# Finishing the rows of two steps' blocks together in the first attention pass of a graph network, and the edge attribute products through two buffers

## Chip, cores and metric

One core of a Trainium2 chip runs the whole program. The metric is the device time of one execution in microseconds; the time before is the median of three runs.

## The reference

A network of four graph layers on 3,125 nodes with 128 features: a graph attention layer with edge attributes, a relational layer, two transformer convolutions, and a two-layer graph convolution. The change touches the first alone. With H = 4 heads of C = 32 columns, E = 103,125 edges, sorted by target, it computes:

```
alpha = leaky_relu(a_src[src] + a_dst[dst] + a_edge, 0.2)     # a_edge from 13 edge attributes
        (and one loop edge per node; its attribute is the mean over the node's edges)
alpha = exp(alpha - segment_max(alpha, dst))
out   = segment_sum(alpha * h[src], dst) / (segment_sum(alpha, dst) + 1e-16)
y     = layernorm(out + bias + x) * gamma + beta
x     = layernorm(x + relu(y))
```

## The kernel before

Nodes lie in NB = 26 blocks of BN = 121 rows, one row to a partition. `attention_pass` is called twice; the first call, named `e0`, has `gat=True` and is the one that the change concerns (the second, `e21`, shares the function). It works in steps. A step takes a chunk of T = 33 tiles of 128 edges, all for one block. With these inputs every block fits one step, so there are 26 steps. Each engine has a loop over 13 pairs of steps, whose body has the two steps u = 0 and u = 1 written out; step s = 2i + u. Here "even step" is u = 0 and "odd step" is u = 1.

In a step the engines do this, tied by semaphores:

- GpSimd (L554) gathers the source rows, 33 indirect DMAs of 128 rows, into `G[:, u]`. There are two such buffers, one per parity of the step. The 33 tiles are in nine batches (`BATCH`); a batch of the step after next may be gathered once TensorE has summed the same batch of this step (`slots_free`).
- SyncE loads the target numbers (`dst3`, and `dstb` over all partitions) and the attributes (`attr`) of the next step once `prepare` of this one is done, and the source numbers of the step after next once the scores are made.
- ScalarE makes the transposed one-hot matrix `OT` of the next step (`one_hot`, L607 and L609) behind the exponential of this step's scores (L617).
- TensorE runs, in this order of its program: the target part of the scores `psQ` of step s (L571, 33 tiles, needs `OT`), six small transposes `psT` (L583), two more `psB` (L588), then the 33 sums `psA` (L594, which need VectorE's weighted rows, L835), and then the `psQ` of step s + 1.
- VectorE waits for the nine gathered batches and for `psQ`, and adds the scores (L790 is the first such instruction of a step). It makes segmented maxima with two scans, subtracts them, weights the gathered rows (L835, nine instructions), runs `prepare` for the next step (L742 to L762), makes the next one-hot matrix `O` (`match`, L766), takes over `psA` (L842), and merges it with the running state `ST` (L845 to L862).

`prepare` ends with the attribute products: for each of four heads a multiplication of 33 x 13 attributes by that head's weights into `pr` (L758) and a sum over 13 (L760), with a drain behind each of the eight.

At the end of each step `finish_block` (L669 to L717) turns `ST` into finished rows of the block: the loop edge's score, the exponential (ScalarE L624), the root for the degree (ScalarE L627), the division, bias, the first `norm` (L648 to L660), gamma, beta, relu, the second `norm`, and the last scaling into `xo[:, u]` (L717). ScalarE takes the roots of both norms, and then stores the rows to the table in memory (L632), after the store before it has landed. Nearly every VectorE instruction there is followed by a drain, since each needs the result of the one before. In a step beyond the last edge or of a block with several steps the same code runs again on the same block.

Of the kernel before, what the change touches and what calls it, by code (L numbers as in the profile page):

```python
# [27 lines left out]
D = 128  # L28
BN = 121
# [413 lines left out]
def attention_pass(g, name, table, width, H, gat):  # L443
# [9 lines left out]
    with ExitStack() as ctx:  # L453
# [28 lines left out]
        if gat:  # L482
            attr = sb("attr", [128, T, 13], F32)
            wed = sb("wed", [128, 13, D])
            atte = sb("atte", [128, D])
            we = sb("we", [128, 4, 13])
            pr = sb("pr", [128, T, 13])
            aff = sb("aff", [BN, 3, D])
            fs = sb("fs", [BN, 20])
            fe = sb("fe", [BN, 8])  # L490
            fy = sb("fy", [BN, D])
            ft = sb("ft", [BN, D])
            fm = sb("fm", [BN, 1])
            fv = sb("fv", [BN, 1])
            fc = sb("fc", [BN, 1])
# [106 lines left out]
        @block.scalar  # L602
        def _(act):
            def one_hot(s):

                act.wait_ge(S["edges_in"], s * (16 * n_in) + 16 * n_in)
                nc.scalar.activation(OT[:], dstb[:], ACT.Square, bias=g["off_t"][0:BN, bass.ds(s, 1)], scale=2.0).then_inc(S["squared"], 1)  # L607
                act.wait_ge(S["squared"], s + 1)
                nc.scalar.activation(OT[:], OT[:], ACT.Relu, bias=one[:], scale=-1.0).then_inc(S["targets_ready"], 1)  # L609

            act.wait_ge(S["one_set"], 1)
            one_hot(0)
            with act.Fori(0, g["n_pairs"](act)) as i:
                for u in range(2):
                    s = i * 2 + u
                    act.wait_ge(S["diff_ready"], s + 1)
                    nc.scalar.activation(G[:, u, :, wo:wo + H].rearrange("p t h -> p h t"), A[:], ACT.Exp).then_inc(S["weights_done"], 1)  # L617
                    act.wait_ge(S["ends_turned"], s + 1)
                    one_hot(s + 1)
                    act.wait_ge(S["merge_ready"], s + 1)  # L620
                    nc.scalar.activation(ex[:], mm[:, 0:2 * H], ACT.Exp).then_inc(S["merge_done"], 1)
                    if gat:
                        act.wait_ge(S["exp_wanted"], s + 1)
                        nc.scalar.activation(fe[:], fs[:, 0:8], ACT.Exp).then_inc(S["exp_made"], 1)  # L624
                        for k, x in enumerate((fc, fv, fv)):
                            act.wait_ge(S["root_wanted"], s * 3 + (k + 1))
                            nc.scalar.activation(x[:], x[:], ACT.Sqrt).then_inc(S["rooted"], 1)  # L627
                        blk = act.value_load(g["steps_i"][0:1, bass.ds(s, 1)], min_val=0, max_val=NB - 1)
                        act.wait_ge(S["row_ready"], s + 1)
                        act.wait_ge(row_stored[1 - u], i * 16 + (16 + 16 * u))  # L630
                        act.sem_inc(S["act_waited"], 1)
                        act.dma_start(g["rows_table"].rearrange("(b p) f -> b p f", p=BN)[bass.ds(blk, 1)].rearrange("a p f -> (a p) f"),  # L632
                                      xo[:, u, :]).then_inc(row_stored[u], 16)
            if gat:
                pairs = g["n_pairs"](act)
                for u in range(2):
                    act.wait_ge(row_stored[u], pairs * 16 + 16)
                    act.sem_inc(S["act_waited"], 1)

        @block.vector  # L640
        def _(dve):
            def bc(x, shape):
                return x.broadcast_to(shape)

            def norm(x, s, count):

                dr = dve.drain
                V.tensor_reduce(fm[:], x, AX.X, ALU.add)  # L648
                dr()
# [12 lines left out]

            def finish_block(s, i, u, blk):

                dr = dve.drain
                plain = D + 2 * H + 1
                q = lambda x, lo, hi: x[:, bass.ds(blk, 1), lo:hi].rearrange("p a f -> p (a f)")
                cnt, al, m, den = ST[:, plain + 4:plain + 5], fs[:, 8:12], fs[:, 12:16], fs[:, 16:20]
                V.tensor_copy(g["deg"][:, bass.ds(blk, 1)], cnt)  # L669
# [4 lines left out]
                V.tensor_tensor(al, q(Q, 0, 4), q(Q, 4, 8), ALU.add)  # L674
                dr()
                V.scalar_tensor_tensor(out=al, in0=ST[:, plain:plain + 4], scalar=fm[:], in1=al, op0=ALU.mult, op1=ALU.add)
                dr()
                V.scalar_tensor_tensor(out=al, in0=al, scalar=0.2, in1=al, op0=ALU.mult, op1=ALU.max)
                dr()
                V.tensor_tensor(m, ST[:, D + H:D + 2 * H], al, ALU.max)  # L680
                dr()
                V.tensor_tensor(fs[:, 0:4], ST[:, D + H:D + 2 * H], m, ALU.subtract)
                V.tensor_tensor(fs[:, 4:8], al, m, ALU.subtract).then_inc(S["exp_wanted"], 1)
                dve.wait_ge(S["rooted"], s * 3 + 1)
                V.reciprocal(g["cnt1"][:, bass.ds(blk, 1)], fc[:])
                dve.wait_ge(S["exp_made"], s + 1)
                V.tensor_tensor(den, ST[:, D:D + H], fe[:, 0:4], ALU.mult)
                dr()
                V.tensor_tensor(den, den, fe[:, 4:8], ALU.add)
                dr()  # L690
                V.tensor_scalar(den, den, 1e-16, None, ALU.add)
                dr()
                V.reciprocal(den, den)
                dr()
                V.tensor_tensor(fe[:].rearrange("p (k h) -> p k h", k=2), fe[:].rearrange("p (k h) -> p k h", k=2),
                                bc(den.unsqueeze(1), [BN, 2, H]), ALU.mult)
                dr()
                hc = lambda x: x.rearrange("p (h c) -> p h c", h=H)
                V.tensor_tensor(hc(fy[:]), hc(ST[:, 0:D]), bc(fe[:, 0:4].unsqueeze(2), [BN, H, C]), ALU.mult)
                V.tensor_tensor(hc(ft[:]), hc(q(g["SKIP"], 0, D)), bc(fe[:, 4:8].unsqueeze(2), [BN, H, C]), ALU.mult)  # L700
                dr()
                V.tensor_tensor(fy[:], fy[:], ft[:], ALU.add)
                dr()
                V.tensor_tensor(fy[:], fy[:], aff[:, 0, :], ALU.add)
                dr()
                V.tensor_tensor(fy[:], fy[:], q(g["X"], 0, D), ALU.add)
                dr()
                norm(fy[:], s, 2)
                V.scalar_tensor_tensor(out=fy[:], in0=fy[:], scalar=fv[:], in1=aff[:, 1, :], op0=ALU.mult, op1=ALU.mult)
                dr()  # L710
                V.tensor_tensor(fy[:], fy[:], aff[:, 2, :], ALU.add)
                dr()
                V.scalar_tensor_tensor(out=fy[:], in0=fy[:], scalar=0.0, in1=q(g["X"], 0, D), op0=ALU.max, op1=ALU.add)
                dr()
                norm(fy[:], s, 3)
                dve.wait_ge(row_stored[u], i * 16 + 16)
                V.tensor_scalar(xo[:, u, :], fy[:], fv[:], None, ALU.mult).then_inc(S["row_ready"], 1)  # L717

            V = nc.vector
            if gat:  # L720
# [16 lines left out]
            def prepare(s, u):  # L737
# [2175 lines left out]
```

## Time and profile before

| | |
|---|---|
| median of 3 runs | 4447.06 us (4443.07 to 4447.44) |
| profiled execution | 4448.53 us, its span 4446.7 us |
| TensorE matmul, weight load busy | 2794.7 us (63%), 2572.4 us (58%) |
| VectorE busy | 3090.5 us (70%) |
| ScalarE busy | 1029.7 us (23%) |
| GpSimd busy | 2741.1 us (62%) |
| mean granted clock of TensorE | 0.736 |

The span is that of one execution, from the first to the last instruction. Busy time is an average over stages with different limits, and the pass `e0` is only one of them: its first gather starts at 58.78 us and its last finished rows are made at 1290.38 us. In the timelines a row gives the start, the duration, the engine, the line, the instruction with what it writes and reads, and in brackets how long the engine stood idle before it and what ended that.

### The profile page before, as it was taken

Reading aid. Unit: us, or ns where it says so; the run is one execution under the profiler, and the core shown is the slowest. Engines: PE = TensorE matmul, PEld = TensorE weight load, DVE = VectorE, ACT = ScalarE, POOL = GpSimd, SP = SyncE. Lnnn points to the kernel's source line nnn. Section 1 sums busy time; section 2 is a strip of 40 time slices with the busy share of each in tenths; the row PEclk is TensorE's granted clock in tenths of the full one; section 3 lists DMA queues with packets and bytes.
Section 4 is the critical chain, followed back from the end, with each engine's and each line's share of the span. In section 5 each row is a group of like instructions: output and inputs, shape, how many; then the busy total and the mean of one; then the engine's idle time right before and its main releaser. Section 6 shows DMA issues by size and latency. Waiting matters only on the chain. (4 is left out here: it accounts for less than half of the span.)

```text
span 4446.7 us, 58830 instructions
## 1 busy us (share of the span) xinstructions
PE 2794.7 (63%) x18074; PEld 2572.4 (58%) x18075; DVE 3090.5 (70%) x7364; ACT 1029.7 (23%) x971; POOL 2741.1 (62%) x2657
## 2 busy tenths in 40 slices
PE   2565656566545565555567465766667657996688
PEld 2565646555534555455556365656656546896566
DVE  3777767777776766666665477777777767997445
ACT  2222222222221222222221121221211213442000
POOL 3777777777627777777772377777777742554000
PEclk7665656565667777777778777877777768998799
DMA  4454444444334445554542455656556533451353
GB/s 108 96 113 99 108 99 97 106 95 111 89 78 118 127 127 136 140 136 136 135 127 80 104 149 145 157 143 153 149 147 154 144 95 93 114 116 37 147 138 91
DMA packets 170486, 526.46 MB, mean 118 GB/s; under 512 B 61894, under 2 KB 88866, under 8 KB 157435
## 3 DMA queue, kind: packets, MB, share of 16 engines
q1 hardware_dynamic: 71532, 297.92, 27.3%
q0 software_dynamic: 95296, 224.30, 19.6%
q8 instruction: 96, 1.57, 0.2%
q10 hardware_dynamic: 3432, 1.61, 0.1%
q14 instruction: 130, 1.06, 0.1%
HBM read 456.16 MB, written 67.48 MB: 118 GB/s over the span
## 5 line engine op out<-in xcount | busy, mean ns | idle before, releaser
L554 POOL DMA_INDIRECT e21G<-table,e21src x858 | 856.4, 998 | 392.2 <-issue 257.8
L554 POOL DMA_INDIRECT e0G<-table,e0src x858 | 863.9, 1007 | 340.1 <-issue 249.8
L1469 POOL DMA_INDIRECT t1G<-table,t1idx x806 | 790.7, 981 | 328.6 <-issue 242.5
L1542 PE MATMUL t1psW<-t1CO,t1G 128*128 128x192 f32 x1612 | 426.0, 426 | 315.3 <-issue 296.9
L1542 PEld LDWEIGHTS t1psW<-t1CO,t1G 128*128 128x128 f32 x1612 | 361.6, 253 | 323.1 <-issue 303.4
L578 PE MATMUL e21psQ<-Q,e21OT 121*128 x1716 | 412.1, 407 | 120.0 <-ACT e21OT L609 44.8
L578 PEld LDWEIGHTS e21psQ<-Q,e21OT 121*128 121x128 f32 x1716 | 400.0, 326 | 131.6 <-issue 86.9
L571 PE MATMUL e0psQ<-Q,e0OT 121*128 x1716 | 398.7, 371 | 78.5 <-ACT e0OT L609 42.4
L571 PEld LDWEIGHTS e0psQ<-Q,e0OT 121*128 121x128 f32 x1716 | 396.6, 325 | 84.0 <-issue 84.0
L2208 POOL TENSOR_TENSOR e22Z<-e22Z,e22C 121x847 f32<-121x847 f32 (+1 forms) x104 | 200.2, 1957 | 257.4 <-ACT e22Z L2200 257.4
L594 PE MATMUL e21psA<-e21G,e21O 128*121 128x145 f32 x1716 | 275.5, 332 | 106.1 <-DVE e21G L835 106.1
L594 PEld LDWEIGHTS e21psA<-e21G,e21O 128*121 128x121 f32 x1716 | 270.4, 224 | 107.8 <-issue 107.8
L594 PE MATMUL e0psA<-e0G,e0O 128*121 128x142 f32 x1716 | 269.2, 328 | 79.8 <-DVE e0G L835 79.8
L594 PEld LDWEIGHTS e0psA<-e0G,e0O 128*121 128x121 f32 x1716 | 263.6, 223 | 82.1 <-DVE e0G L835 82.1
L1781 DVE TENSOR_TENSOR t1AT<-t1AT,t1psW 128x192 f32 x186 | 64.9, 349 | 311.7 <-PE t1psW L1542 311.2
L784 DVE TENSOR_TENSOR e21G<-e21psQ,e21G 128x512 f32<-128x512 f32 (+1 forms) x234 | 150.2, 642 | 153.4 <-DMA e21G<-table,e21src 121.2
L1699 DVE TENSOR_TENSOR t1L<-t1psI,RES 128x1089 f16<-128x1089 f32 (+1 forms) x182 | 226.9, 1247 | 0.0
L1504 PEld LDWEIGHTS t1psN<-SKIP,t1L 128*121 128x121 f16 x1586 | 137.5, 167 | 153.9 <-issue 149.2
L1504 PE MATMUL t1psN<-SKIP,t1L 128*121 128x52 f16 x1586 | 143.8, 238 | 125.7 <-issue 124.4
L583 PE MATMUL e0psT<-eye,e0TI 128*4 128x128 f32 x156 | 37.4, 411 | 283.0 <-DVE e0TI L811 283.0
L1662 DVE TENSOR_TENSOR t1CO<-t1OW,t1psC 128x960 f32<-128x960 f32 x186 | 189.8, 1021 | 20.9 <-issue 10.7
L583 PEld LDWEIGHTS e0psT<-eye,e0TI 128*4 128x4 f32 x156 | 15.6, 113 | 294.1 <-DVE e0TI L811 285.3
(423 smaller groups left out, 5432.1 us busy)
## 6 DMA issues: line engine op xcount, KB each, us to landing
e0dstb<-in_dst_p SPq DMA_DIRECT2D x27, 1996.5 KB
e21dstb<-in_dst_p SPq DMA_DIRECT2D x27, 1996.5 KB
e22C<-counts SPq DMA_DIRECT2D x26, 1487.0 KB
llC<-planes SPq DMA_DIRECT2D x52, 743.5 KB
Q<-in_type_p SPq DMA_DIRECT2D x62, 416.0 KB
counts<-X SPq DMA_DIRECT2D x13, 1487.0 KB
planes<-SKIP SPq DMA_DIRECT2D x26, 743.5 KB
counts<-RES SPq DMA_DIRECT2D x13, 1487.0 KB
```

What stands on the lines that cost most here:

```text
L554: nc.gpsimd.indirect_dma_start(out=G[:, u, t, 0:width], out_offset=None, in_=table, in_offset=bass.IndirectOffsetOnAxis(ap=src[:, u, t:t + ...
L571: mmi = nc.tensor.matmul(psQ[:, u, t * QW:(t + 1) * QW], onehot[:, t, :], Q[:, bass.ds(blk, 1), 0:QW].rearrange("p a f -> p (a f)"), start ...
L578: mmi = nc.tensor.matmul(psQ[:, b % 3, j * QW:(j + 1) * QW], onehot[:, t, :], Q[:, bass.ds(blk, 1), 0:QW].rearrange("p a f -> p (a f)"), s ...
L594: mmi = nc.tensor.matmul(psA[0:BN, 0:NC], O[:, t, :], G[:, u, t, vo:vo + NC], start=(t == 0), stop=(t == T - 1))
L784: V.tensor_tensor(G[:, u, t0:t1, 0:D], q, G[:, u, t0:t1, 0:D], ALU.mult).then_inc(S["spread_free"], 1)
L1469: nc.gpsimd.indirect_dma_start(out=G[:, q % 2, t, :], out_offset=None, in_=table, in_offset=bass.IndirectOffsetOnAxis(ap=idx[:, q * GT + t ...
L1504: mmi = nc.tensor.matmul(psN[0:BN, c % 2, i * 2 * NB:(i + 1) * 2 * NB], L[:, c % 2, i, :], K[:, c % 2, i, :], start=True, stop=True)
L1542: mmi = nc.tensor.matmul(psW[:, k % 2, 0:WIN * NBAS], G[:, q % 2, t, :], CO[:, k % 2, i].rearrange("p b w -> p (b w)"), start=(i == 0), st ...
L1662: V.tensor_tensor(CO[:, k % 2, 0:n], OW[:, u, t0:t0 + n, :].unsqueeze(2).broadcast_to([128, n, NBAS, WIN]), made.unsqueeze(3).broadcast_to ...
L1699: V.tensor_tensor(L[:, c % 2, 0:m, :], iol.unsqueeze(1).broadcast_to([128, m, BN]), lb.unsqueeze(2).broadcast_to([128, m, BN]), ALU.is_equ ...
L1781: V.tensor_tensor(to, to, psW[:, k % 2, 0:WIN * NBAS].rearrange("p (b w) -> p b w", b=NBAS), ALU.add).then_inc(S["added"], 1)
L2208: nc.gpsimd.tensor_tensor(Z[:, u, h0:h1, :], Z[:, u, h0:h1, :], C[:, u, h0:h1, :], ALU.mult).then_inc(S["weighted"], 1)
```

## The change

Two edits, both inside `attention_pass` with `gat=True`.

First, `finish_block` becomes `finish_blocks`, called once per pair. At the end of each step VectorE copies `ST` into a half of a new tile `two`. Behind the odd step, after a drain, it loads both block numbers into registers and finishes both blocks. Where operands lie side by side one instruction covers both halves (tiles `fs`, `fd`, `fx`, `fn`, `fe`, `fy`, `ft`, `fm`, `fv`, `fc` get a dimension of 2); where an operand is addressed by block number, or a scalar per row is used, there are two instructions. The fused loop-edge score (L676) becomes a product and a sum, and `cnt1` is now written from `fc` by two copies. ScalarE does one exponential and three roots per pair, and both stores at the end of the odd step.

Second, the attribute products go through two buffers `pr[:, 0]` and `pr[:, 1]`: head h is multiplied and, without a drain between, head h - 1 is summed; one drain follows each such pair, and the last sum has none behind it. In the diff below the removed body of `finish_block`, which is printed above, and the sizes of the other small tiles are left out.

```diff
--- before.py
+++ after.py
@@ -484,15 +484,19 @@
-            pr = sb("pr", [128, T, 13])
+            pr = sb("pr", [128, 2, T, 13])
...
+            two = sb("two", [BN, 2, NC])
+            fs = sb("fs", [BN, 2, 8])
...
@@ -619,16 +623,18 @@
                     one_hot(s + 1)
                     act.wait_ge(S["merge_ready"], s + 1)
                     nc.scalar.activation(ex[:], mm[:, 0:2 * H], ACT.Exp).then_inc(S["merge_done"], 1)
-                    if gat:
-                        act.wait_ge(S["exp_wanted"], s + 1)
-                        nc.scalar.activation(fe[:], fs[:, 0:8], ACT.Exp).then_inc(S["exp_made"], 1)
-                        for k, x in enumerate((fc, fv, fv)):
-                            act.wait_ge(S["root_wanted"], s * 3 + (k + 1))
-                            nc.scalar.activation(x[:], x[:], ACT.Sqrt).then_inc(S["rooted"], 1)
-                        blk = act.value_load(g["steps_i"][0:1, bass.ds(s, 1)], min_val=0, max_val=NB - 1)
-                        act.wait_ge(S["row_ready"], s + 1)
+                if gat:
+                    act.wait_ge(S["exp_wanted"], i + 1)
+                    nc.scalar.activation(fe[:], fs[:], ACT.Exp).then_inc(S["exp_made"], 1)
+                    for k, x in enumerate((fc, fv, fv)):
+                        act.wait_ge(S["root_wanted"], i * 3 + (k + 1))
+                        nc.scalar.activation(x[:], x[:], ACT.Sqrt).then_inc(S["rooted"], 1)
+                    act.wait_ge(S["row_ready"], i + 1)
+                    for u in range(2):
+
                         act.wait_ge(row_stored[1 - u], i * 16 + (16 + 16 * u))
                         act.sem_inc(S["act_waited"], 1)
+                        blk = act.value_load(g["steps_i"][0:1, bass.ds(i * 2 + u, 1)], min_val=0, max_val=NB - 1)
                         act.dma_start(g["rows_table"].rearrange("(b p) f -> b p f", p=BN)[bass.ds(blk, 1)].rearrange("a p f -> (a p) f"),
                                       xo[:, u, :]).then_inc(row_stored[u], 16)
             if gat:
@@ -642,79 +648,95 @@
             def bc(x, shape):
                 return x.broadcast_to(shape)
 
-            def norm(x, s, count):
+            def norm(x, i, count):
 
                 dr = dve.drain
                 V.tensor_reduce(fm[:], x, AX.X, ALU.add)
                 dr()
                 V.tensor_scalar(fm[:], fm[:], 1.0 / D, None, ALU.mult)
                 dr()
-                V.tensor_scalar(x, x, fm[:], None, ALU.subtract)
+                V.tensor_tensor(x, x, bc(fm[:].unsqueeze(2), [BN, 2, D]), ALU.subtract)
                 dr()
                 V.tensor_tensor(ft[:], x, x, ALU.mult)
                 dr()
                 V.tensor_reduce(fv[:], ft[:], AX.X, ALU.add)
                 dr()
                 V.tensor_scalar(fv[:], fv[:], 1.0 / D, EPS, ALU.mult, ALU.add).then_inc(S["root_wanted"], 1)
-                dve.wait_ge(S["rooted"], s * 3 + count)
+                dve.wait_ge(S["rooted"], i * 3 + count)
                 V.reciprocal(fv[:], fv[:])
                 dr()
 
-            def finish_block(s, i, u, blk):
...
+            def finish_blocks(i):
 
                 dr = dve.drain
                 plain = D + 2 * H + 1
+                blks = [dve.value_load(g["steps_i"][0:1, bass.ds(i * 2 + u, 1)], min_val=0, max_val=NB - 1) for u in range(2)]
+                q = lambda x, u, lo, hi: x[:, bass.ds(blks[u], 1), lo:hi].rearrange("p a f -> p (a f)")
+                cnt = two[:, :, plain + 4:plain + 5].rearrange("p k a -> p (k a)")
+                tops = two[:, :, D + H:D + 2 * H]
+                wide = lambda x: bc(x.unsqueeze(2), [BN, 2, H])
+                V.tensor_copy(g["deg"][:, bass.ds(blks[0], 1)], two[:, 0, plain + 4:plain + 5])
                 V.tensor_scalar(fc[:], cnt, 1.0, None, ALU.add).then_inc(S["root_wanted"], 1)
                 V.tensor_scalar(fm[:], cnt, 1.0, None, ALU.max)
+                for u in range(2):
+                    V.tensor_tensor(fn[:, u, :], q(Q, u, 0, 4), q(Q, u, 4, 8), ALU.add)
                 dr()
                 V.reciprocal(fm[:], fm[:])
+                V.tensor_copy(g["deg"][:, bass.ds(blks[1], 1)], two[:, 1, plain + 4:plain + 5])
+                dr()
+                V.tensor_tensor(fd[:], two[:, :, plain:plain + 4], wide(fm[:]), ALU.mult)
+                dr()
+                V.tensor_tensor(fn[:], fn[:], fd[:], ALU.add)
+                dr()
+                V.scalar_tensor_tensor(out=fn[:], in0=fn[:], scalar=0.2, in1=fn[:], op0=ALU.mult, op1=ALU.max)
+                dr()
+                V.tensor_tensor(fx[:], tops, fn[:], ALU.max)
+                dr()
+                V.tensor_tensor(fs[:, :, 0:4], tops, fx[:], ALU.subtract)
+                V.tensor_tensor(fs[:, :, 4:8], fn[:], fx[:], ALU.subtract).then_inc(S["exp_wanted"], 1)
+                dve.wait_ge(S["rooted"], i * 3 + 1)
+                V.reciprocal(fc[:], fc[:])
+                dr()
+                V.tensor_copy(g["cnt1"][:, bass.ds(blks[0], 1)], fc[:, 0:1])
+                dve.wait_ge(S["exp_made"], i + 1)
+                V.tensor_tensor(fd[:], two[:, :, D:D + H], fe[:, :, 0:4], ALU.mult)
+                dr()
+                V.tensor_copy(g["cnt1"][:, bass.ds(blks[1], 1)], fc[:, 1:2])
+                V.tensor_tensor(fd[:], fd[:], fe[:, :, 4:8], ALU.add)
+                dr()
+                V.tensor_scalar(fd[:], fd[:], 1e-16, None, ALU.add)
+                dr()
+                V.reciprocal(fd[:], fd[:])
+                dr()
+                for k in range(2):
+                    V.tensor_tensor(fe[:, :, k * 4:k * 4 + 4], fe[:, :, k * 4:k * 4 + 4], fd[:], ALU.mult)
                 dr()
                 hc = lambda x: x.rearrange("p (h c) -> p h c", h=H)
+                for u in range(2):
+                    V.tensor_tensor(hc(fy[:, u, :]), hc(two[:, u, 0:D]), bc(fe[:, u, 0:4].unsqueeze(2), [BN, H, C]), ALU.mult)
+                    V.tensor_tensor(hc(ft[:, u, :]), hc(q(g["SKIP"], u, 0, D)), bc(fe[:, u, 4:8].unsqueeze(2), [BN, H, C]), ALU.mult)
                 dr()
                 V.tensor_tensor(fy[:], fy[:], ft[:], ALU.add)
                 dr()
+                V.tensor_tensor(fy[:], fy[:], bc(aff[:, 0, :].unsqueeze(1), [BN, 2, D]), ALU.add)
+                dr()
+                for u in range(2):
+                    V.tensor_tensor(fy[:, u, :], fy[:, u, :], q(g["X"], u, 0, D), ALU.add)
+                dr()
+                norm(fy[:], i, 2)
+                for u in range(2):
+                    V.scalar_tensor_tensor(out=fy[:, u, :], in0=fy[:, u, :], scalar=fv[:, u:u + 1], in1=aff[:, 1, :], op0=ALU.mult, op1=ALU.mult)
+                dr()
+                V.tensor_tensor(fy[:], fy[:], bc(aff[:, 2, :].unsqueeze(1), [BN, 2, D]), ALU.add)
+                dr()
+                for u in range(2):
+                    V.scalar_tensor_tensor(out=fy[:, u, :], in0=fy[:, u, :], scalar=0.0, in1=q(g["X"], u, 0, D), op0=ALU.max, op1=ALU.add)
+                dr()
+                norm(fy[:], i, 3)
+                for u in range(2):
+                    dve.wait_ge(row_stored[u], i * 16 + 16)
+                    mmi = V.tensor_scalar(xo[:, u, :], fy[:, u, :], fv[:, u:u + 1], None, ALU.mult)
+                mmi.then_inc(S["row_ready"], 1)
 
             V = nc.vector
             if gat:
@@ -755,10 +777,11 @@
                 if gat:
 
                     for h in range(4):
-                        V.tensor_tensor(pr[:], attr[:], bc(we[:, h:h + 1, :], [128, T, 13]), ALU.mult)
+                        V.tensor_tensor(pr[:, h % 2], attr[:], bc(we[:, h:h + 1, :], [128, T, 13]), ALU.mult)
+                        if h:
+                            V.tensor_reduce(G[:, u, :, GW - 6 + h:GW - 5 + h].rearrange("p t a -> p (t a)"), pr[:, 1 - h % 2], AX.X, ALU.add)
                         dve.drain()
-                        V.tensor_reduce(G[:, u, :, GW - 5 + h:GW - 4 + h].rearrange("p t a -> p (t a)"), pr[:], AX.X, ALU.add)
-                        dve.drain()
+                    V.tensor_reduce(G[:, u, :, GW - 2:GW - 1].rearrange("p t a -> p (t a)"), pr[:, 1], AX.X, ALU.add)
                 V.memset(X1[:], 0.0).then_inc(S["edges_used"], 1)
 
             def match(t0, t1):
@@ -771,7 +794,8 @@
             with dve.Fori(0, g["n_pairs"](dve)) as i:
                 for u in range(2):
                     s = i * 2 + u
-                    blk = dve.value_load(g["steps_i"][0:1, bass.ds(s, 1)], min_val=0, max_val=NB - 1)
+                    if not gat:
+                        blk = dve.value_load(g["steps_i"][0:1, bass.ds(s, 1)], min_val=0, max_val=NB - 1)
                     sc = bass.ds(s, 1)
                     for b, tiles in enumerate(BATCH):
                         n = len(tiles)
@@ -863,9 +887,12 @@
                                                in1=acc[:, NC - 5:NC], op0=ALU.mult, op1=ALU.add)
                     dve.drain()
                     if gat:
-                        finish_block(s, i, u, blk)
+                        V.tensor_copy(two[:, u, :], ST[:])
                     else:
                         V.tensor_copy(RES[:, bass.ds(blk, 1), 0:NC].rearrange("p a f -> p (a f)"), ST[:])
+                if gat:
+                    dve.drain()
+                    finish_blocks(i)
             dve.drain()
 
 
```

## Rows read from the trace of the kernel before

**Rows 1.** The page's busy time of each engine, share of the span, instructions.

```profile
PE 2794.7 (63%) x18074; PEld 2572.4 (58%) x18075; DVE 3090.5 (70%) x7364; ACT 1029.7 (23%) x971; POOL 2741.1 (62%) x2657
```

**Rows 2.** Timeline of VectorE: L790 in steps 0, 1, 11, 12 and 25, of 26.

```profile
110.34 0.38 DVE L790 TENSOR_TENSOR e0A<-e0psQ,e0G 128x132 f32<-128x132 f32 x1 [15.61 <-DMA e0G<-table,e0src]
154.17 0.38 DVE L790 TENSOR_TENSOR e0A<-e0psQ,e0G 128x132 f32<-128x132 f32 x1 [0.69 <-issue]
...
610.90 0.38 DVE L790 TENSOR_TENSOR e0A<-e0psQ,e0G 128x132 f32<-128x132 f32 x1 [0.70 <-issue]
658.46 0.38 DVE L790 TENSOR_TENSOR e0A<-e0psQ,e0G 128x132 f32<-128x132 f32 x1 [4.45 <-issue]
...
1247.85 0.38 DVE L790 TENSOR_TENSOR e0A<-e0psQ,e0G 128x132 f32<-128x132 f32 x1 [0.93 <-issue]
```

**Rows 3.** Timeline of GpSimd: gathers 33, 34, 66, 298 and 463 of 858.

```profile
103.32 0.94 POOL L554 DMA_INDIRECT e0G<-table,e0src  x1 [0.31 <-issue]
104.57 0.95 POOL L554 DMA_INDIRECT e0G<-table,e0src  x1 [0.30 <-issue]
...
146.16 0.94 POOL L554 DMA_INDIRECT e0G<-table,e0src  x1 [0.30 <-issue]
...
445.32 0.96 POOL L554 DMA_INDIRECT e0G<-table,e0src  x1 [0.30 <-issue]
...
671.95 2.13 POOL L554 DMA_INDIRECT e0G<-table,e0src  x1 [4.20 <-PE e0psA L594]
```

**Rows 4.** Timeline of VectorE: attribute products, one-hot and finish of step 11.

```profile
627.23 0.60 DVE L758 TENSOR_TENSOR e0pr<-e0attr,e0we 128x429 f32<-128x429 f32 x1
627.90 0.60 DVE L760 TENSOR_REDUCE e0G<-e0pr 128x33 f32<-128x429 f32 x1
...
632.71 0.17 DVE L762 MEMSET e0X<- 128x132 f32 x1
632.80 4.83 DVE L766 TENSOR_TENSOR e0O<-iota,e0dstf 128x484 f32<-128x484 f32 x9
...
640.58 0.15 DVE L669 COPY deg<-e0ST 121x1 f32 x1 [0.15 <-issue]
...
644.24 0.16 DVE L685 RECIPROCAL cnt<-e0fc 121x1 f32 x1 [1.88 <-ACT e0fc L627]
...
645.75 0.29 DVE L699 TENSOR_TENSOR e0fy<-e0ST,e0fe 121x128 f32<-121x128 f32 x1
645.96 0.29 DVE L700 TENSOR_TENSOR e0ft<-SKIP,e0fe 121x128 f32<-121x128 f32 x1
646.32 0.29 DVE L702 TENSOR_TENSOR e0fy<-e0fy,e0ft 121x128 f32<-121x128 f32 x1
...
653.65 0.36 DVE L717 TENSOR_SCALAR e0xo<-e0fy,e0fv 121x128 f32<-121x128 f32 x1
```

**Rows 5.** Timeline of TensorE: psA and psQ in step 12, psA in another.

```profile
668.91 10.27 PE L594 MATMUL e0psA<-e0G,e0O 128*121 128x142 f32 x66 [3.07 <-DVE e0G L835]
680.43 15.34 PE L571 MATMUL e0psQ<-Q,e0OT 121*128 x66 [1.24 <-issue]
...
850.94 9.72 PE L594 MATMUL e0psA<-e0G,e0O 128*121 128x142 f32 x66 [3.07 <-DVE e0G L835]
```

**Rows 6.** Timelines of VectorE, ScalarE's queue and SyncE's at the pass's end.

```profile
1290.10 0.28 DVE L717 TENSOR_SCALAR e0xo<-e0fy,e0fv 121x128 f32<-121x128 f32 x1
1290.70 0.55 ACTq L632 DMA_DIRECT2D table<-e0xo  x1
1293.36 0.34 SPq L1412 DMA_DIRECT2D t1idx<-in_src_cols  x1
```

**Rows 7.** TensorE in two stretches of step 12's psQ: us, busy, granted clock, DMA.

```profile
680.40:682.40 2.00, 1.97 (x9) 1.00 0.60 127
690.40:695.80 5.40, 5.37 (x24) 0.50 0.76 166
```

More of the change, by code:

```diff
@@ L486, in attention_pass @@
             we = sb("we", [128, 4, 13])
-            pr = sb("pr", [128, T, 13])
+            pr = sb("pr", [128, 2, T, 13])
             aff = sb("aff", [BN, 3, D])
[L489 to L495, printed above, removed]
+            two = sb("two", [BN, 2, NC])
+            fs = sb("fs", [BN, 2, 8])
+            fd = sb("fd", [BN, 2, 4])
+            fx = sb("fx", [BN, 2, 4])
+            fn = sb("fn", [BN, 2, 4])
+            fe = sb("fe", [BN, 2, 8])
+            fy = sb("fy", [BN, 2, D])
+            ft = sb("ft", [BN, 2, D])
+            fm = sb("fm", [BN, 2])
+            fv = sb("fv", [BN, 2])
+            fc = sb("fc", [BN, 2])
             xo = sb("xo", [BN, 2, D])
@@ L658, in norm @@
                 V.tensor_scalar(fv[:], fv[:], 1.0 / D, EPS, ALU.mult, ALU.add).then_inc(S["root_wanted"], 1)
-                dve.wait_ge(S["rooted"], s * 3 + count)
+                dve.wait_ge(S["rooted"], i * 3 + count)
                 V.reciprocal(fv[:], fv[:])
                 dr()
-            def finish_block(s, i, u, blk):
+            def finish_blocks(i):
                 dr = dve.drain
                 plain = D + 2 * H + 1
-                q = lambda x, lo, hi: x[:, bass.ds(blk, 1), lo:hi].rearrange("p a f -> p (a f)")
-                cnt, al, m, den = ST[:, plain + 4:plain + 5], fs[:, 8:12], fs[:, 12:16], fs[:, 16:20]
-                V.tensor_copy(g["deg"][:, bass.ds(blk, 1)], cnt)
+                blks = [dve.value_load(g["steps_i"][0:1, bass.ds(i * 2 + u, 1)], min_val=0, max_val=NB - 1) for u in range(2)]
[4 more added lines that the diff above has]
+                V.tensor_copy(g["deg"][:, bass.ds(blks[0], 1)], two[:, 0, plain + 4:plain + 5])
@@ L670, in finish_block @@
                 V.tensor_scalar(fc[:], cnt, 1.0, None, ALU.add).then_inc(S["root_wanted"], 1)
                 V.tensor_scalar(fm[:], cnt, 1.0, None, ALU.max)
+                for u in range(2):
+                    V.tensor_tensor(fn[:, u, :], q(Q, u, 0, 4), q(Q, u, 4, 8), ALU.add)
                 dr()
                 V.reciprocal(fm[:], fm[:])
-                V.tensor_tensor(al, q(Q, 0, 4), q(Q, 4, 8), ALU.add)
+                V.tensor_copy(g["deg"][:, bass.ds(blks[1], 1)], two[:, 1, plain + 4:plain + 5])
@@ L675, in finish_block @@
                 dr()
-                V.scalar_tensor_tensor(out=al, in0=ST[:, plain:plain + 4], scalar=fm[:], in1=al, op0=ALU.mult, op1=ALU.add)
+                V.tensor_tensor(fd[:], two[:, :, plain:plain + 4], wide(fm[:]), ALU.mult)
                 dr()
-                V.scalar_tensor_tensor(out=al, in0=al, scalar=0.2, in1=al, op0=ALU.mult, op1=ALU.max)
+                V.tensor_tensor(fn[:], fn[:], fd[:], ALU.add)
                 dr()
-                V.tensor_tensor(m, ST[:, D + H:D + 2 * H], al, ALU.max)
+                V.scalar_tensor_tensor(out=fn[:], in0=fn[:], scalar=0.2, in1=fn[:], op0=ALU.mult, op1=ALU.max)
@@ L681, in finish_block @@
                 dr()
[L682 to L687, printed above, removed]
-                dr()
-                V.tensor_tensor(den, den, fe[:, 4:8], ALU.add)
@@ L690, in finish_block @@
-                dr()
-                V.tensor_scalar(den, den, 1e-16, None, ALU.add)
-                dr()
-                V.reciprocal(den, den)
-                dr()
-                V.tensor_tensor(fe[:].rearrange("p (k h) -> p k h", k=2), fe[:].rearrange("p (k h) -> p k h", k=2),
-                                bc(den.unsqueeze(1), [BN, 2, H]), ALU.mult)
+                V.tensor_tensor(fx[:], tops, fn[:], ALU.max)
+                dr()
+                V.tensor_tensor(fs[:, :, 0:4], tops, fx[:], ALU.subtract)
@@ L700, in finish_block @@
-                V.tensor_tensor(hc(ft[:]), hc(q(g["SKIP"], 0, D)), bc(fe[:, 4:8].unsqueeze(2), [BN, H, C]), ALU.mult)
+                for u in range(2):
+                    V.tensor_tensor(hc(fy[:, u, :]), hc(two[:, u, 0:D]), bc(fe[:, u, 0:4].unsqueeze(2), [BN, H, C]), ALU.mult)
+                    V.tensor_tensor(hc(ft[:, u, :]), hc(q(g["SKIP"], u, 0, D)), bc(fe[:, u, 4:8].unsqueeze(2), [BN, H, C]), ALU.mult)
                 dr()
@@ L703, in finish_block @@
                 dr()
-                V.tensor_tensor(fy[:], fy[:], aff[:, 0, :], ALU.add)
+                V.tensor_tensor(fy[:], fy[:], bc(aff[:, 0, :].unsqueeze(1), [BN, 2, D]), ALU.add)
                 dr()
-                V.tensor_tensor(fy[:], fy[:], q(g["X"], 0, D), ALU.add)
-                dr()
-                norm(fy[:], s, 2)
-                V.scalar_tensor_tensor(out=fy[:], in0=fy[:], scalar=fv[:], in1=aff[:, 1, :], op0=ALU.mult, op1=ALU.mult)
+                for u in range(2):
+                    V.tensor_tensor(fy[:, u, :], fy[:, u, :], q(g["X"], u, 0, D), ALU.add)
+                dr()
+                norm(fy[:], i, 2)
+                for u in range(2):
+                    V.scalar_tensor_tensor(out=fy[:, u, :], in0=fy[:, u, :], scalar=fv[:, u:u + 1], in1=aff[:, 1, :], op0=ALU.mult, op1=ALU.mult)
                 dr()
-                V.tensor_tensor(fy[:], fy[:], aff[:, 2, :], ALU.add)
+                V.tensor_tensor(fy[:], fy[:], bc(aff[:, 2, :].unsqueeze(1), [BN, 2, D]), ALU.add)
                 dr()
-                V.scalar_tensor_tensor(out=fy[:], in0=fy[:], scalar=0.0, in1=q(g["X"], 0, D), op0=ALU.max, op1=ALU.add)
-                dr()
-                norm(fy[:], s, 3)
-                dve.wait_ge(row_stored[u], i * 16 + 16)
-                V.tensor_scalar(xo[:, u, :], fy[:], fv[:], None, ALU.mult).then_inc(S["row_ready"], 1)
+                for u in range(2):
+                    V.scalar_tensor_tensor(out=fy[:, u, :], in0=fy[:, u, :], scalar=0.0, in1=q(g["X"], u, 0, D), op0=ALU.max, op1=ALU.add)
+                dr()
+                norm(fy[:], i, 3)
[3 more added lines that the diff above has]
+                mmi.then_inc(S["row_ready"], 1)
             V = nc.vector
```

1 line of the change is left out of this document (removed).

## The prediction

> **What bounds the kernel now.** I read the views in this order: the page, to see which engines are busy; the timeline of VectorE over the first attention pass, to see the rhythm of its steps; the timeline of GpSimd, to see how far ahead the gathers are; TensorE inside one step; and the end of the pass.
>
> The page alone decides nothing: VectorE is busy 70% and GpSimd 62% of the span [rows 1]. The change touches one stage, the pass "e0", so it has to be read there. It runs 26 steps in 13 loop iterations of two; L790, the first VectorE instruction that uses a step's gathered rows, marks each step. It starts at 110.34 us in step 0 and at 1247.85 in step 25 [rows 2]. The distance alternates. From an even step to the odd one behind it are 43.8 to 43.9 us (110.34 to 154.17). From an odd step to the next even one, across the return of the loop, are 47.6 (610.90 to 658.46). Thirteen of the first kind at 43.9 leave (1137.5 - 13 x 43.9) / 12 = 47.2 for the second: a pair costs 91.1 us.
>
> Who sets that? Not the gathers: 264 of them (8 steps) take from 104.57 to 445.32, 42.6 us a step, 85.2 a pair, as long as nothing holds them; later GpSimd stands 4.20 us waiting for a free buffer, released by TensorE's psA matmuls [rows 3]. Before L790 VectorE idles only 0.70 us in odd steps. In even steps it idles 4.45, and no engine is named for it ("issue"), right behind the return of the loop [rows 2]. So VectorE itself is the bound, in every step from the first, and what it saves is saved until the next limit is met.
>
> **The next limit.** TensorE has a chain through every step. Step 12 starts at 658.46 [rows 2]; its psA matmuls start at 668.91, released by the first weighted rows (L835), and last 10.27 us; then come the psQ matmuls of step 13, at 680.43, for 15.34 us, to 695.77 [rows 5]. L790 of step 13 needs them. So two neighbouring steps can't be closer than 695.77 - 658.46 = 37.3 us. This follows from program order: psQ(s+1) stands behind psA(s), and psA(s) behind VectorE's step s. psA took 9.72 in another step [rows 5], so I give the chain 36.8 to 38. The psQ matmuls pass at the same pace at either clock: 9 in 2.00 us at a granted clock of 1.00, 24 in 5.40 at 0.50 [rows 7]; a shift of the clock won't shorten them.
>
> **The change part by part.**
>
> *Finishing rows in even steps.* It goes, with its wait for ScalarE. It lasts from L669 to the end of L717: 640.58 to 654.01, 13.4 us, of which 1.88 is the wait for the exponential, the table load and the root [rows 4]. In its place stands one copy of 142 columns, some 0.3.
>
> *Attribute products.* Before, eight instructions, each followed by a drain, run from 627.23 to 632.71: 5.5 us, 0.67 from start to start [rows 4]. After, seven of the eight remain in pairs without a drain between. Undrained starts follow at 4.83 / 9 = 0.54 for 484 columns (L766), so about 0.49 for 429. The sum is 0.68 + 3 x (0.49 + 0.68) + 0.49 = 4.7: a saving of 0.8 us per step.
>
> The step L758 to L760 shows what a drain adds: 0.67 against a duration of 0.60 [rows 4]. The Trainium skill, "VectorE: DVE Perf Modes", section "The DRAIN you can't avoid", says that one cannot skip the pipeline flush by chaining operations without semaphores. By it the 0.8 would be 0. The rows disagree: L700 starts 0.21 us behind L699, whose duration is 0.29 [rows 4].
>
> *VectorE in even steps after.* 43.9 - 13.4 - 0.8 + 0.3 = 30.0 us. That is below TensorE's 37.3. So of 13.9 us saved only 43.9 - 37.3 = 6.6 are had, and 7.3 become a new wait of L790 on psQ in odd steps.
>
> *Finishing both blocks in odd steps.* Before 39 instructions, after 51. Doubling a 128-column operation in one instruction adds 128 columns at 0.54 / 484 = 1.1 ns, 0.14 us. Eleven are doubled so (the sum with the skip, bias, beta, and four in each of two norms): 1.5. Six wide ones are issued twice (four products instead of two, the second sum with X, gamma, relu, the last scaling); undrained a second costs 0.21 [rows 4], with its register addresses up to 0.3: 1.5. Another six or seven small ones (the split fused operation, two copies for cnt1 with a drain, the second sum of Q, the second degree copy) add some 1.1. Together 4.1. Bounds: below, 1.5 and twelve starts at the smallest spacing of these rows, 0.09 (L762 to L766 [rows 4]), 2.6; above, each extra instruction as if drained, 0.37 for the six wide ones (645.96 to 646.32) and, less 128 columns at 1.1 ns, 0.23 for seven small ones, 5.3. I take 4.1, because most extra instructions stand beside an independent twin. The waits for ScalarE stay one each, so the 1.88 is paid once for two blocks.
>
> The copy with its drain and the two register loads that now stand in front of the finish add about 0.6. Odd step after: 47.2 - 0.8 + 4.1 + 0.6 = 51.1. The stall at the loop's return is kept at its size.
>
> *Stores.* Both stores now follow one another on ScalarE's queue, the second only when the first has landed. In the last pair this delays the end: issue to the next phase's first DMA is 1293.36 - 1290.70 = 2.7 us [rows 6], the upper bound of one landing, so I add 2.7 (0 to 2.7). In the other pairs ScalarE's table load and the exponential of the next step queue behind it; their result is used just before psA starts, 668.91 - 654.01 = 14.9 us behind the finish [rows 4, 5], and two stores at 2.7 and a table load (it is a part of the 1.88) take at most 7.3. Hidden; without cover it would be at most 2.7 a pair.
>
> *Gathers.* First even period: gather(1)'s last instruction starts at 146.16 [rows 3]. In step 0 it took 110.34 - 103.32 = 7.0 us from the last gather to L790, so L790(1) comes at 153.2, a period of 42.9. From there a pair takes 37.3 + 51.1 = 88.4, over the gathers' 85.2, so they run ahead again and are no limit.
>
> **Sum.** Before, from L790 of step 0 to the end of the last L717 (1290.10 + 0.28 [rows 6]): 1180.0 us. After: 42.9 + 12 x 51.1 + 12 x 37.3 + the last step (42.5 - 0.8 + 4.1 + 0.6 = 46.4) = 1150.1. Plus 2.7: a gain of 27 us. All later phases start behind a barrier, and shift. The profiled execution took 4448.53 (span 4446.7), 1.5 above the median of 4447.06; so 4448.5 - 27 = 4421.5, and against the median 4420. I say **4421**.
>
> **Rivals.** (About 0.2%, 9 us, is what a measurement of this kernel can tell from no change.)
>
> 1. *The gathers become the bound.* It would need the even period, TensorE's chain, at 85.2 - 51.1 = 34.1 or less. Then step 25 starts at 104.57 + 24 x 42.6 + 41.6 + 7.0 = 1175.6, the pass ends at 1222.0, 68.4 earlier, less 2.7: 4383. For it: gathers are only 3.2 us a pair under my limit. Against: the chain is plain program order. Chance 0.10.
> 2. *The joint finish is as dear as the upper bound.* 5.3 instead of 4.1, and 0.1 more for the registers: 1.3 x 13 = 17 us of the gain go, 4438, just at the 9 us. Chance 0.18, half of it faster by over 0.2%.
> 3. *Slower.* The place is the joint finish. At the loop's return VectorE loses 4.45 - 0.70 = 3.75 us to no engine [rows 2]. If the finish, now longer and behind two register loads, met such a stall a second time, each odd step would be 54.9 and the last 50.2: 13 x 3.75 = 49 us against a gain of 27, so 4470. It decides from 27 / 13 = 2.1 us per pair on. For it: the margin is small, and even steps can't pay it, because TensorE holds them. Against: nothing like it stands inside a step now. Chance 0.13.
> 4. *Undrained instructions save nothing.* The 0.8 is lost in 13 odd steps, and in the finish some 1.3 more: 27 us, no change, 4448. The page named above says it; the 0.21 of L700 speaks against it. Chance 0.02.
>
> My forecast has 0.57. The range 4392 to 4448 holds it with its own bounds (2.6 instead of 4.1 gives 4402; 37.8 instead of 37.3 gives 4427) and rival 2. Faster: 0.57 + 0.10 + 0.09 of rival 2 = 0.76; same 0.09 + 0.02 = 0.11; slower 0.13.
>
> **What will show it.** L790 waits some 7 us for psQ in odd steps, L790 periods alternate 37.3 and 51; psQ(s+1)'s end and L790(s+1) coincide; ScalarE's table loads in the pass halve; the finish takes about 17.5 us per pair; L758 to L762 takes 4.7. The prediction is wrong if odd L790 are released by gathers, if the finish passes 19.6, or if VectorE's idle time at the loop's return moves by more than 1 us.

## The result, and the profile after

The changed kernel takes 4554.43 us (median of 4) against 4446.26: a ratio of 1.0251, 95% interval 1.0238 to 1.0264. It is 108 us slower; the profiled execution took 4553.47 us, its span is 4551.7. I had said 4421, faster. The page after has VectorE less busy (3090.5 before [rows 1]), as the edits meant, and another row that I hadn't looked at: the queue of instruction fetches. Its columns are packets, MB and share of the DMA engines; before it had 130 packets, 1.06 MB.

```profile
PE 2805.2 (62%) x18074; PEld 2585.9 (57%) x18075; DVE 3027.7 (67%) x7039; ACT 985.8 (22%) x893; POOL 2748.8 (60%) x2657
...
q14 instruction: 188, 1.54, 0.1%
```

The first pass after, read as [rows 2] (L790 is now L814), steps 0, 1, 11, 12, 13 and 25:

```profile
111.28 0.38 DVE L814 TENSOR_TENSOR e0A<-e0psQ,e0G 128x132 f32<-128x132 f32 x1 [17.09 <-DMA e0G<-table,e0src]
153.15 0.38 DVE L814 TENSOR_TENSOR e0A<-e0psQ,e0G 128x132 f32<-128x132 f32 x1 [12.56 <-DMA e0G<-table,e0src]
...
613.33 0.38 DVE L814 TENSOR_TENSOR e0A<-e0psQ,e0G 128x132 f32<-128x132 f32 x1 [7.45 <-PE e0psQ L575]
667.30 0.38 DVE L814 TENSOR_TENSOR e0A<-e0psQ,e0G 128x132 f32<-128x132 f32 x1 [5.59 <-issue]
704.68 0.38 DVE L814 TENSOR_TENSOR e0A<-e0psQ,e0G 128x132 f32<-128x132 f32 x1 [8.25 <-PE e0psQ L575]
...
1253.52 0.38 DVE L814 TENSOR_TENSOR e0A<-e0psQ,e0G 128x132 f32<-128x132 f32 x1 [9.02 <-PE e0psQ L575]
```

TensorE holds the odd steps, as forecast: 704.68 - 667.30 = 37.4, and the idle time is named psQ. But the way back over the loop's return takes 53.97 (613.33 to 667.30; mean of 12: 53.75), not 51.1. From the first L814 to the end of the last finish (1301.08) are 1189.8 us, 9.8 more than before instead of 30 less.

That is a tenth of the loss. The rest lies where no line was changed. These are VectorE's rows at one return of the loop in the *second* pass, e21, before and after: the last instruction of an odd step, and the first of the next even one.

```profile
2618.09 0.24 DVE L868 COPY RES<-e21ST 121x145 f32 x1 [0.17 <-issue]
2619.45 0.69 DVE L784 TENSOR_TENSOR e21G<-e21psQ,e21G 128x512 f32<-128x512 f32 x1 [1.12 <-issue]
```

```profile
2630.31 0.24 DVE L892 COPY RES<-e21ST 121x145 f32 x1 [0.17 <-issue]
2646.97 0.69 DVE L808 TENSOR_TENSOR e21G<-e21psQ,e21G 128x512 f32<-128x512 f32 x1 [16.43 <-issue]
```

VectorE stands 16.43 us where it stood 1.12, at each of the 12 returns (15.5 to 16.6), and "issue" means that the profile names no engine and no DMA that it waited for. The DMA view of the same stretch (2450 to 3700 us), before and after, has the fetches:

```profile
q14 instruction: 11, 0.09, 0.0%
```

```profile
q14 instruction: 68, 0.56, 0.2%
```

57 more of 8 KB in 12 returns, some five each. Three of the five lie inside the idle time. At the return shown, VectorE's branch ends at 2630.47 us. Packets of this queue start at 2635.41, 2637.69 and 2644.18 us, and the first register load of the body starts at 2646.14 us (times of the trace's own records; the timeline leaves out branches and register loads).

The account of the whole loss: the pass e0 +9.8, its end to the next phase +3.3, e21 (first L808 to the last copy to RES: 1119.9 to 1210.2) +90.3, all else +1.7: 105.1 of span.

### The profile page after: what moved, and what is told of

It is laid out like the page before. It is cut to its first block and busy times, and to the rows that moved or that the text cites. A ratio compares the mean times of both kernels' runs of the same rounds, so it can differ in the third digit from the quotient of the medians.

```text
span 4551.7 us, 57929 instructions
## 1 busy us (share of the span) xinstructions
PE 2805.2 (62%) x18074; PEld 2585.9 (57%) x18075; DVE 3027.7 (67%) x7039; ACT 985.8 (22%) x893; POOL 2748.8 (60%) x2657
## 5 line engine op out<-in xcount | busy, mean ns | idle before, releaser
L808 DVE TENSOR_TENSOR e21G<-e21psQ,e21G 128x512 f32<-128x512 f32 (+1 forms) x234 | 150.2, 642 | 244.4 <-issue 201.0
L621 ACT ACTIVATE e21G<-e21A 128x264 f32<-128x264 f32 x26 | 17.4, 668 | 812.1 <-DVE e21A L851 812.1
```

The costliest lines, as they stand in the source:

```text
L808: V.tensor_tensor(G[:, u, t0:t1, 0:D], q, G[:, u, t0:t1, 0:D], ALU.mult).then_inc(S["spread_free"], 1)
```

## Experiments

Theory F: VectorE fetches its instructions in pieces of 8 KB; at the return of a loop it finds the body's start on the chip only if the body touches few enough pieces, and that depends on where the body begins in the instruction stream. A body that is found there is called resident. The change took 65 instructions out ahead of the second pass and so moved a loop that it never touched. The rival, P: the second pass is slower through something that the first one does.

All paddings are drains in front of VectorE's work in a pass, while it waits for its first loads:

```
V = nc.vector
+for _ in range(n_first if gat else n_second):
+    dve.drain()
```

**The loop of the second pass back in its place** (change, n_second = 65).

> The changed kernel with 65 drains put in front of VectorE's work in the second attention pass, while it waits for its first loads. That puts the second pass's VectorE loop back at the place in VectorE's instruction stream that it had before the change (the change took 65 instructions out of what stands ahead of it). Theory F (instruction fetch: whether the return of a loop finds its first instructions still on the chip depends on where the body lies): the 16 us of idle time at the return of the second pass's loop fall to about 1 us, 92 us of the 105 lost come back, 4462 us. Rival P (the second pass is slower because of what the first pass leaves or when it ends: timing, data placement): no change, 4554 us. The first pass keeps its time by both.

4454.09 us, ratio 1.0020 (1.0010 to 1.0029), 8 us under the 4462 expected. The wait at the return is 1.12 again:

```profile
2631.47 0.69 DVE L810 TENSOR_TENSOR e21G<-e21psQ,e21G 128x512 f32<-128x512 f32 x1 [1.12 <-issue]
```

Rival P falls.

**The kernel before, moved into the bad place** (n_second = 63).

> The kernel before the change with 63 drains in front of VectorE's work in the second attention pass, nothing else. Its loop then begins at the same place within a piece of 128 instructions as in the changed kernel. Theory F with pieces of 128: the stall of 16 us appears at each return of the second pass's loop, +92 us, about 4539. With pieces of 256 it would not have to appear. Rival P: no change, 4447.

4549.13 us, ratio 1.0231 (1.0214 to 1.0248). Sixty-three drains alone do nearly as much harm as the whole change:

```profile
2635.96 0.69 DVE L786 TENSOR_TENSOR e21G<-e21psQ,e21G 128x512 f32<-128x512 f32 x1 [16.42 <-issue]
```

**The change with 30 drains ahead of the first pass** (n_first = 30).

> The changed kernel with 30 drains in front of VectorE's work in the first attention pass, in the 16 us in which it waits for its constants. All later loops move by 30 instructions. Theory F, read with the fetches that the trace shows (8 KB each, so 128 instructions if one has 64 bytes, and five of them per loop return): both loop bodies, 337 and 268 instructions, then lie so that they touch one such piece fewer (three, not four); idle time at both loop returns falls, in the first pass from 5.5 to about 1 us (55 us over 12 returns), in the second by 92 us in all: about 4405 us, faster than before the change. If F holds but a body of 337 is always too long: 4462. Rival P: 4554.

4395.71 us, ratio 0.9891 (0.9875 to 0.9908): faster than both kernels, by 1.1% than the kernel before. The return of the first pass's loop waits 0.63 us instead of 5.59, and in the stretch from 200 to 1180 us, where the kernel before has 53 fetches, none is left.

```profile
675.37 0.38 DVE L816 TENSOR_TENSOR e0A<-e0psQ,e0G 128x132 f32<-128x132 f32 x1 [7.50 <-PE e0psQ L575]
724.13 0.38 DVE L816 TENSOR_TENSOR e0A<-e0psQ,e0G 128x132 f32<-128x132 f32 x1 [0.63 <-issue]
```

**How few drains are enough** (n_first = 4, and 12).

> The changed kernel with only 4 drains in front of the first pass's VectorE work. Theory F: the first pass's body then begins where it began in the kernel before and in the joint finish alone, where a body of 345 was resident; a body of 337 must be too, so the stall at its return goes (55 us). The second pass's body moves by 4 within its piece; the runs so far leave open whether that takes it out of the last 11 places: 4396 if it does, 4490 if not. If the length of padding matters and not the place: close to 4554.

> The changed kernel with 12 drains in front of the first pass's VectorE work. Theory F: the second pass's body then begins where it did in the joint finish alone, without a stall, and the first pass's 8 places further on than there, still within three pieces: 4396, as with 30 drains. If four or twelve drains are too few: 4450 to 4554.

4399.23 us (0.9899, 0.9883 to 0.9916) and 4397.94 us (0.9897, 0.9880 to 0.9913). Four instructions that do nothing are worth 155 us in the changed kernel: both bodies began at most four places too early.

**One edit at a time.** The attribute products alone (in the kernel before: `pr` of two halves, and the sum of head h - 1 behind the product of head h, as in the diff):

> The kernel before with the attribute products through two buffers alone. The step that the prediction put at 0.8 us, on the path of VectorE in every one of 26 steps here, since finishing stays in each step: 21 us faster, 4426. If undrained pairs save nothing: 4447. Theory F: the loop of the second pass begins at place 2 instead of 14 of a piece of 128, which should not matter; a loss of 92 us here would say that the rule is another.

4465.87 us, ratio 1.0042 (1.0026 to 1.0059): slower, where 4426 was expected. The step itself is 0.75 us shorter (43.92 to 43.17 from even to odd steps), but the return waits 6.9 us on average instead of 4.1, and in 200 to 1180 us there are 63 fetches instead of 53: six a return instead of five.

```profile
760.53 0.38 DVE L791 TENSOR_TENSOR e0A<-e0psQ,e0G 128x132 f32<-128x132 f32 x1 [7.06 <-issue]
...
q14 instruction: 63, 0.52, 0.2%
```

The same with n_first = 4:

> The attribute products alone with 4 drains in front of the first pass's VectorE work, so that its body of 390 begins where the body of the kernel before does. Theory F: instead of six fetches per return five, as before, and the stall of 7.0 us returns to about 4.1: 35 us less than the attribute products alone without drains, 4431, and 16 to 20 faster than before the change, which is the 0.75 us per step that the edit saves. If the edit itself causes the longer stall: 4466.

4441.84 us, ratio 0.9987 (0.9977 to 0.9996): the wait is 4.0 us again, with 52 fetches, so the longer stall was a matter of place and not of the edit. The gain is 5 us by the medians, not the 16 to 20 expected. The pass is 13.8 us shorter (1166.2 against 1180.0), but these are two single profiled executions, 12.3 us apart in all (4436.28 and 4448.53), the first of them well under its median. The step from even to odd takes 43.32 us here, 0.6 less than before.

The joint finish alone (the diff without its attribute hunk), and with n_first = 28:

> The kernel before with the joint finish alone (attribute products as before). Theory F by places: the second pass's loop begins 12 instructions further on within its piece of 128 than in the changed kernel. From the runs so far a body of 268 is resident unless it begins in the last 11 places of a piece, and the changed kernel's begins there; so here no stall of 16 us, and the first pass (345 instructions, at a place where they touch four pieces) keeps its stall: about 4472, some 80 us faster than the whole change although one of its two edits, a good one, is missing. If instead the joint finish by itself causes the second pass's loss: about 4560.

> As the run before, with 28 drains in front of the first pass's VectorE work. Theory F: the body of 345 then touches three pieces, the stalls at both loops' returns are gone: the first pass's even-to-odd periods stay at 38 (TensorE), the odd-to-even ones are 48.6 + 0.75. About 10 us slower than the whole change with 30 drains, 4405: that is what the attribute edit is worth by itself once the finish is joint. If the attribute edit saves nothing on the path: 4396.

4400.96 us (0.9891, 0.9875 to 0.9908) and 4401.69 us (0.9898, 0.9882 to 0.9915). I had expected the first pass's stall to stay in the former; it was gone. Its `pr` code ahead of the loop is four instructions longer, which puts the body at place 69, where the table below has it resident. So the joint finish alone gained 48 us, most of it through the stall (see below), and the second edit, harmless in itself, moved both bodies into bad places. What the attribute edit adds once the finish is joint and no stall is left isn't shown: the ratios, 0.9898 without it and 0.9891 with it, have overlapping intervals, and the pass in the two profiles is 3.1 us shorter (1131.2 to 1128.1), where 10 were expected.

**The kernel before, n_first = 30.**

> The kernel before with 30 drains in front of the first pass's VectorE work. Theory F: 398 instructions touch four or five pieces wherever they begin, so the stall at the first pass's return stays, but its length depends on the place: 4.1 us before, 7.0 with the attribute edit alone, 5.5 with the whole change. So between 3.5 and 7.5 per return, 4440 to 4487; the second pass unchanged, at 1 us. If padding itself helped or hurt, all would move by the same amount whatever the body: a stall near 1 us here would refute the count of pieces.

4448.94 us, ratio 1.000 (0.999 to 1.001): 398 instructions keep their stall (4.0 to 4.6 us).

**Register loads moved into TensorE's wait** (change, n_first = 30, and in the step loop `elif u: blks = [value_load ...]`, no longer inside `finish_blocks`).

> The changed kernel with 30 drains, and the two register loads of the block numbers moved from in front of the joint finish to the start of the odd step, where VectorE waits some 8 us for psQ. The 1.5 us that VectorE idles ahead of the finish fall to a few tenths: 1.3 us in each of 13 pairs, 17 us less than with the 30 drains alone, about 4379, if the gathers (85.2 a pair against 85.3 then) don't take over. If the idle time is the drain's and not the loads': 4396.

4392.46 us (0.9875, 0.9858 to 0.9891): 3 us less than with the 30 drains alone, not 17, and with intervals that overlap. From odd to even steps it is 1.4 us shorter (48.64 to 47.24), but from even to odd 1.4 longer (37.96 to 39.32), since gathers now release 10 of the 13 odd L817 (5 of 13 with the loads in their old place):

```profile
932.94 0.38 DVE L817 TENSOR_TENSOR e0A<-e0psQ,e0G 128x132 f32<-128x132 f32 x1 [10.36 <-DMA e0G<-table,e0src]
```

My rival 1 has come true there, at 86.6 us a pair: the gathers' steady pace, counted over the whole pass, is nearer 86 than the 85.2 of their first steps [rows 3]. It is close in the other five runs without stalls as well (the joint finish alone, also with 28 drains; the change with 4, 12 and 30 drains). In all six a pair takes 86.5 to 86.9 us and the last gather ends at 1177.0 to 1178.7 us; in the kernel before it ended at 1213.4. GpSimd's waits in the pass, before and with 30 drains (total us, times, longest):

```profile
POOL e0G L554 <- PE e0psA L594: 39.1, 35, 4.2
```

```profile
POOL e0G L558 <- issue: 251.1, 824, 0.3
POOL e0G L558 <- PE e0psA L598: 9.8, 32, 0.3
```

GpSimd no longer waits for a buffer longer than the 0.3 us that stand between any two gathers. Step 1 starts 3.8 to 5.2 us behind its last gather and step 25 starts 11.5 to 17.1 us behind its own, so a faster VectorE could have had no more than some 7 to 12 us of this pass (an estimate). That is why neither the attribute edit nor the moved loads bring their full price.

**All places together.** A place is the number of instructions that stand ahead of the loop's body in VectorE's built program, modulo 128. Stalls are the mean idle time at a return in us ("no" is 0.6 in the first pass and 1.1 in the second); "fetches" are packets per return.

| run | first pass: place, length | stall, fetches | second pass: place (268 long) | stall |
|---|---|---|---|---|
| before | 69, 398 | 4.1, 5 | 14 | no |
| change | 65, 337 | 5.6, 5 | 77 | 16.1 |
| + 65 in second | 65, 337 | 5.6, 5 | 14 | no |
| before + 63 in second | 69, 398 | 4.2, 5 | 77 | 16.4 |
| change + 4, 12, 30 in first (30 also with the loads moved) | 69, 77, 95, 337 | no, 0 | 81, 89, 107 | no |
| finish only, + 28 | 69, 97, 345 | no, 0 | 89, 117 | no |
| attributes only | 65, 390 | 6.9, 6 | 2 | no |
| attributes only + 4 | 69, 390 | 4.0, 5 | 6 | no |
| before + 30 in first | 99, 398 | 4.3, 5 | 44 | no |

One rule fits every row. Take pieces of 128 instructions, with an edge between places 65 and 69 in the first pass and between 77 and 81 in the second. A body that touches three pieces stays on the chip. One that touches four or more is fetched again at each return, all its pieces and one more (four give five; the one case of five gives six). The edges are fitted, one for each pass; why they differ isn't known. The size is not free: with pieces of 256, a body of 268 could touch one more piece from 11 places only, and it stalled at two places 128 apart (77 and 205, modulo 256).

The Trainium skill, "Runtime: NRT & Kernel Launch", section "Instruction fetch mechanics", says the same in kind: a taken branch whose target is outside the current two-page window forces a fetch, and pages have 16 KiB. The packets here have 8 KB (0.56 MB in 68), and the two places just named speak against pages of twice that size on this engine; the measurement decides for smaller pieces. The prediction didn't draw on this.

## Why the prediction was wrong

*The step that failed:* "The stall at the loop's return is kept at its size", and with it "All later phases start behind a barrier, and shift". I saw 3.75 us lost to no engine [rows 2], the profile's "issue", and asked neither what it was nor what the change does to it. In the first pass it grew from 4.1 to 5.6 us a return. In the second, whose loop the change doesn't touch, it went from 1.1 to 16.1. It depends on place and length of the code, so a change of 65 instructions reaches every later loop. The second pass's +90 us were in no term and no rival; rival 3 had the right kind of cost in the wrong place, and its 49 us were too few. The last sign that I had given for being wrong, idle time at the return moving by more than 1 us, did show it.

*What held.* The chain of TensorE: 37.4 in the pair above, mean of 12 after the first: 37.9 against 37.3. VectorE's new wait on psQ: 7.5 to 9.1 us against 7.3, in 11 of 13 odd steps; the first two wait for gathers (12.56 and 10.63 us), of which I had counted one. ScalarE's table loads halved, 26 instead of 52. The joint finish, start to end in the last pair (rows between them left out):

```profile
1269.75 1.28 DVE L780 TENSOR_TENSOR e0pr<-e0attr,e0we 128x429 f32<-128x429 f32 x2
...
1274.58 0.17 DVE L785 MEMSET e0X<- 128x132 f32 x1
...
1282.05 0.22 DVE L886 SCALAR_TENSOR_TENSOR e0ST<-e0ST,keep_t,e0acc 121x5 f32<-121x5 f32 x1
1282.35 0.23 DVE L890 COPY e0two<-e0ST 121x142 f32<-121x142 f32 x1
1284.13 0.15 DVE L678 COPY deg<-e0two 121x1 f32 x1 [1.54 <-issue]
...
1300.60 0.48 DVE L738 TENSOR_SCALAR e0xo<-e0fy,e0fv 121x128 f32<-121x128 f32 x2
```

The finish takes 1301.08 - 1284.13 = 16.95 us (I said 17.5), the attribute products 4.8 (4.7). Mis-sized was what stands in front: 1284.13 - 1282.27 = 1.86 us against 0.15 before [rows 4], where I had 0.6; moving the loads away took 1.4 off the odd step, so most of it was the register loads behind the drain. The two stores in a row cost 3.3 at the end (first DMA of the next phase 6.3 us behind the finish, 3.0 before [rows 6]); I said 2.7.

*The sum for the first pass.* 1189.8 against 1150.1. The missing 39.7: odd-to-even periods 12 x 2.65 = 31.8, of which the longer stall 1.5 each and the register loads 1.1 or so; even-to-odd 6.7; last step 1.2. The stall alone doesn't explain this pass. From even to odd steps 6.0 us are saved (43.92 to 37.95), where I had 6.6. From odd to even 6.5 are lost (47.22 to 53.75), 1.45 of them by the longer stall and 5.1 by the finish and its loads, where I had 3.9. So a pair saves 0.9 us besides the stall and not 2.7: the gain was a small difference of two large terms, and both were a little off.

Without the stalls (30 drains) the pass takes 1128.1, 52 us less than before. Most of that isn't the mechanism that I forecast either: 12 x (4.12 - 0.63) = 42 us are the stall itself, which is gone because a body of 337 instructions can lie in three pieces and one of 398 can't. That leaves, as an estimate, 10 us for the joint finish and the attribute products, where I had 30 for this pass. The fetches both turned the change into a loss and, with the padding, make up most of its gain.

*Rivals.* 4 (undrained pairs save nothing) is refuted by 0.75 and 0.6 us a step in the two runs of the attribute products alone. 2 is not the case: the finish took 16.95 us. 1 isn't the case in the changed kernel, where GpSimd still waits for buffers. It comes true with the register loads moved, and is within some 12 us in the other runs without stalls.

## What to carry to other kernels

Idle time of an engine at a loop's return, with no releaser, is a cost with a cause: look at the instruction queue's packets per return before you take it as fixed. An edit that adds or removes instructions moves the code of every later loop on that engine, so compare all phases, not the edited one; if an untouched loop has changed, pad by a few instructions and measure again before you judge the edit. A body that is just over an edge is worth shortening or moving first: here 4 drains took back 155 us, and of the 52 us that the first pass gained in the end some 42 came from the shorter body. When a cost goes that held one engine, look at once at the next limit: here the gathers were then within 1 us a pair.

## What was not expected of the hardware

The stall's length isn't the number of fetches alone: five fetches cost 4 to 5.6 us at a return in the first pass and 16 in the second. In the second, the fetches fall into a stretch in which the gathers and the large target load (2.0 MB) keep the DMA engines busy: at the return shown their share is 0.88 from 2630.4 to 2635.4 us and 0.75 from there to 2646.1, while the fetches come in at 2635 to 2636, 2637 to 2638 and 2644 to 2645 us. At a return of the first pass (661.4 to 667.3 us) the share is 0.33. That this is the reason is argued from these returns; no run tried it.
